# The vector engine takes its turns at the wide PSUM bank one product later

## What is computed

```python
# layer 0: x = e, xk = e;  layers 1 and 2: x = e, xk = the sum of the layer before, the same for all 256 columns
z = jnp.einsum('bfe,bge->bfge', x, xk).reshape(B, 256, E)
z = relu(einsum('bcl,oc->bol', z', Ws[i]) + bs[i])      # 16 outputs o for each column
z = sum(z, axis=-1)                                      # (B, 16)
h = concatenate([z of the three layers, dense_ctx])      # (2048, 64)
h = relu(h @ W_top1 + b_top1); h = relu(h @ W_top2 + b_top2); y = h @ W_top3
```

## Time and profile before

| what | value |
|---|---|
| time, median of 3 runs | 611.44 us (611.04 to 613.63) |
| the profiled execution | 614.28 us, span 612.5 us |
| granted TensorE clock, mean of the span | 0.989 |
| PE busy | 566.3 us, 92% |
| DVE busy | 494.5 us, 81% |
| ACT busy | 437.6 us, 71% |
| POOL busy | 463.1 us, 76% |

### The profile page before, as it was taken

How to read it: one execution, slowest core, us unless ns; L and a number is a source line. 1 busy time by engine, 2 the same in 40 slices (tenths; PEclk the granted TensorE clock), 3 DMA queues, 4 the chain that set the end, 5 groups by cost and what they waited for, 6 DMA issues and landing times.

```text
span 612.5 us, 18145 instructions
## 1 busy us (share of the span) xinstructions
PE 566.3 (92%) x7680; PEld 329.1 (54%) x7680; DVE 494.5 (81%) x220; ACT 437.6 (71%) x1234; POOL 463.1 (76%) x565
## 2 busy tenths in 40 slices
PE   1778889999999999999999999999999999999776
PEld 1334445555555565655556555555556565555444
DVE  5898899888888988888889888888899888887100
ACT  2466677768778776878878777887877786886542
POOL 5989888888878887888878888888878788862000
PEclk9999899999999999999999999999999999999978
DMA  4422222222222222222222122222222222210000
GB/s 98 115 76 73 62 62 71 61 62 63 61 62 63 61 63 63 61 63 61 63 63 65 58 64 62 60 63 61 63 64 63 68 61 59 59 45 1 1 1 2
DMA packets 14788, 35.89 MB, mean 59 GB/s; under 512 B 5921, under 2 KB 6305, under 8 KB 14689
## 3 DMA queue, kind: packets, MB, share of 16 engines
q0 software_dynamic: 12288, 33.57, 19.3%
q1 hardware_dynamic: 2418, 1.16, 0.8%
HBM read 34.70 MB, written 0.01 MB: 57 GB/s over the span
## 4 chain that ended last, share of the span: by engine, by line
PE 68%; DVE 20%; issue 7%; ACT 3%; POOL 2%; DMA 0%; SPq 0%; DVEq 0%; POOLq 0%; ACTq 0%
PE sum_ps L521 29%; DVE prods L222 19%; PE turn_ps L501 9%; PE outer_ps L564 9%; PE wide_ps L585 7%; PE sum_ps L541 5%; PE wide_ps L576 4%; PE outer_ps L559 3%; ACT relu_k L431 2%; POOL emb L262 2%; PE sum_ps L536 1%; PE wide_ps L593 1%; PE sum_ps L547 0%; PE sum_ps L533 0%; DMA id_lim<-id_limits 0%
## 5 line engine op out<-in xcount | busy, mean ns | idle before, releaser
L222 DVE TENSOR_TENSOR prods<-turn_ps,emb_t 128x3360 f32<-128x3360 f32 x128 | 462.2, 3646 | 11.8 <-ACT emb_t L404 8.9
L262 POOL DMA_INDIRECT emb<-tables,rows_sb x256 | 252.1, 985 | 44.9 <-issue 31.1
L521 PE MATMUL sum_ps<-prods,w_sb 128*32 128x272 f32 x4096 | 267.1, 400 | 2.5 <-POOL prods L222 2.3
L521 PEld LDWEIGHTS sum_ps<-prods,w_sb 128*32 128x32 f32 x4096 | 126.0, 110 | 94.0 <-issue 14.5
L421 ACT ACTIVATE relu<-sum_ps,bias_sb 128x120 f32<-128x120 f32 x256 | 91.8, 370 | 100.8 <-PE sum_ps L521 96.6
L272 POOL TENSOR_TENSOR prods<-emb_t 128x256 f32<-128x256 f32 x128 | 94.8, 741 | 53.8 <-ACT emb_t L404 50.3
L431 ACT ACTIVATE relu_k<-outer_ps 128x2048 f32<-128x2048 f32 x64 | 120.9, 1889 | 4.5 <-PE outer_ps L564 4.4
L501 PE MATMUL turn_ps<-ident_sb,emb 128*128 128x128 f32 x512 | 90.7, 295 | 29.7 <-DVE prods L222 10.9
L403 ACT COPY emb_t<-turn_ps 128x512 f32<-128x512 f32 x128 | 76.1, 595 | 44.2 <-PE turn_ps L501 36.2
L501 PEld LDWEIGHTS turn_ps<-ident_sb,emb 128*128 128x128 f32 x512 | 55.1, 143 | 88.8 <-issue 49.0
L411 ACT ACTIVATE prods<-emb_t 128x512 f32<-128x512 f32 x128 | 83.0, 649 | 0.1
(11 more groups left out here) (41 smaller groups left out, 269.2 us busy)
## 6 DMA issues: line engine op xcount, KB each, us to landing
emb<-tables,rows_sb POOLq DMA_INDIRECT x256
w_sb<-w_top SPq DMA_DIRECT2D x1, 512.0 KB
ids_sb<-ids_t SPq DMA_DIRECT2D x1, 128.0 KB, 2.0
h<-dense_t SPq DMA_DIRECT2D x1, 128.0 KB
w_sb<-w_top SPq DMA_DIRECT2D x1, 128.0 KB
ident_sb<-ident SPq DMA_DIRECT2D x1, 64.0 KB
w_sb<-w_cols SPq DMA_DIRECT2D x1, 64.0 KB
wp_sb<-w_proj SPq DMA_DIRECT2D x1, 32.0 KB
```

The costliest lines, as they stand in the source:

```text
L222: eng.tensor_tensor(out, every, shifted, ALU.mult).then_inc(done, 1)
L262: nc.gpsimd.indirect_dma_start(out=emb[:, k % EMB_RING, t * E:(t + 1) * E], out_offset=None, in_=tables, in_offset=bass.IndirectOffsetOnAx ...
L521: last = nc.tensor.matmul(sum_ps[s * 2 * F:(s + 1) * 2 * F, 0:SUM_COLS], w_sb[:, c, odd, :], x[:, c, 2 * s + odd, :, :], start=c == 0 and ...
```

## The change

Two constants are raised by one slot. `turn_proj(g)` stands after `products` of slot 12 instead of slot 11, `reduce_fields(0, g)` after that of slot 16 instead of 15, and `reduce_fields(1, g)` after that of slot 21 instead of 20. No instruction is added or taken away, and no other engine's program is touched; what each semaphore counts is the same.

```diff
-PROJ, Z0_FIN, TURN_P, Z0_DIAG, Z0_SUM = 10, 9, 11, 9, 10
+PROJ, Z0_FIN, TURN_P, Z0_DIAG, Z0_SUM = 10, 9, 12, 9, 10
 Z_BUILD = (11, 15)
 ROUNDS = (12, 16)
 FOLD = (14, 19)
-REDUCE = (15, 20)
+REDUCE = (16, 21)
```

## The result

The changed kernel took 623.82 us (median of 4 runs, 623.65 to 624.13) against 611.76 for the kernel before in the same series (4 runs, 611.04 to 613.63): ratio 1.0193, 95% interval 1.0169 to 1.0217, 12.1 us slower. The forecast was 618.3: 623.8 lies inside its range, but the loss was put too small, 6.8 us against 12.1. The profiled execution has a span of 622.0 us, 9.5 more than the profile of before; that one profile lay above all of its runs (614.28 us against 611.04 to 613.63), which is why the medians are further apart than the spans.

A forecast was written before the change was run, and what follows sets the result against it. The prediction took TensorE to bound the kernel: 10.1 us lost in groups 1 to 14 less 3.3 gained in group 0 is 6.8 us slower, 611.44 + 6.8 = 618.3 us, range 609.5 to 625.

The forecast's parts named there:

- What bounds the kernel: Whole kernel: TensorE, busy 92% of the span, sets the time; the DVE's large waits belong to an engine with time to spare.
- The wait that takes the place of the one removed: Slots 11 and 15: TensorE's last sum matmul waits for the wide bank; slot 11's release at 376.03, slot 15's at 393.26.
- Slot 11, net 0.77 us: Slot 11, groups 1 to 14: new wait of 0.93 us for the transpose, less the old 0.16 us in slot 12.
- Slot 15, net -0.05: Slot 15, groups 1 to 13: new wait of 0.26 us for the sum, less the old 0.31 us in slot 16.
- No slack elsewhere: Middle groups: neither new wait feeds on slack that an earlier one made, since ScalarE's copies hang on TensorE's sums.
- Sum of groups 1 to 14: Groups 1 to 14: 13 x 0.72 + 0.77 = 10.1 us lost, bounds 3.8 and 15.5 us.
- Group 0: Group 0: gaps of 1.82 and 1.80 us and slow sums (1.69 us) go; 3.3 us gained, bounds 1.8 and 5.3.
- The limit that I named there: Group 0: POOL reaches 82.9 us, and the sums of slot 17 can't start before that, which limits the 5.31 us gain.
- POOL's late spread: Slot 15: POOL's `z_spread(1, g)` waits some 2 us longer for the moved sum; cost zero, without cover up to 1 us a group.
- the second sum: Slot 20 to 21: the sum is ready before its first reader either way; cost and gain zero, without cover 0.42 us a group.
- (1): Rival, slots 11 and 15: new waits don't bite and only the old ones go; 9.6 us faster, 601.8; chance 0.10.
- (3): Rival, sums after the new wait: TensorE's clock falls, 1.69 us per set in 14 groups; 30.5 us slower, 642; chance 0.04.

The follow-up runs named there:

- the second pair of profiles: The kernel before and the changed kernel, both unchanged, run and profiled once more on one chip: 611.84 us and 623.47 us.

## Why the prediction was right, and where it was too small

- **What bounds the kernel**: right. TensorE's order does; the DVE's waits for TensorE before the transposes and the sums fell from 84.5 to 31.4 us in all, and the kernel got no faster.
- **The wait that takes the place of the one removed**: right in place and in time. The release in slot 11 was put at 376.03 on a slot that began at 372.87, 3.16 us into it; it was 379.41 - 376.25 = 3.16. The copy of ScalarE, the product and the transpose set it.
- **Slot 11, net 0.77 us**: too small, 1.01 measured. This is the term that was mis-sized. I had counted the wait from 375.1, the start of the last batch of matmuls, on the ground that "the array is free" after it. But the held matmul has a pass in each of the last two batches; in the trace of before its first pass starts at 374.87 and its second at 375.10. The first is what is held: it moved from 374.87 - 372.87 = 2.00 us into the slot to 3.16, by 1.16 us and not 0.93. The fold is cut into the same column groups and shifts with it: it started 3.17 us into the slot instead of 2.44, 0.73 late, and then took 2.29 us to the next turn instead of 1.85, another 0.44; together 1.17, less the old wait of 0.16 that is 1.01. With the wait moved behind the sums the 0.44 vanished (5.46 to 5.02 us), which shows it. My upper bound by the weights, 0.97, was nearer.
- **Slot 15, net -0.05**: it was +0.15. Here too I had taken the second pass (393.0); the first started at 392.77, 2.40 us into the slot, and now starts 2.89 us into it, 0.49 late. The sums end 0.52 us late, against 0.26 in the forecast, and the old wait was 4.41 - 4.04 = 0.37, not 0.31. With the wait behind the sums no wait was left at all.
- **No slack elsewhere**: slots 16 to 18 gave back 0.15 us, which I had not seen.
- **Sum of groups 1 to 14**: 10.1 forecast, 12.7 in the trace. **Group 0**: 3.3 forecast, 3.38 in the trace. The limit that I named there held: POOL's last blocks of step 17 end at 82.68 us against my 82.9, and the sums of slot 17 start at 82.79 (both rows stand above). On the way TensorE waited 0.62 us in slot 12 and 1.00 us in slot 16 for ScalarE's reading of the sums, which I had not seen; POOL, which had no gap from 66.4 us on, would have held it back without them. But that the gain came out at 3.3 is in part luck: 1.69 us of it were the slow sums, which the second pair of profiles does not have (1.85 us gained).
- **The median**: 6.8 us forecast, 12.1 measured. Of the 5.3 us missing, the trace of the first pair has 2.7 (9.5 us between the spans). The rest lies between that profile of before and its median, 614.28 against 611.76 us: I took the gain of group 0 from an execution with slow sums and added it to the median of executions most of which may not have had them. The second pair fits this, with 1.85 us gained in group 0 and 11.4 us between the spans; how many of the timed executions have the slow sums isn't on record.
- **POOL's late spread, the second sum, the tail**: nothing, as said. The run with the second sum alone shows 0; no run has the late spread alone, but TensorE's matmuls of line 521 wait for POOL only once in the whole span, 2.6 us at the start (2.3 before).
- **The rivals**: (1) needed a release 1.1 us earlier and did not occur. (3) did not occur: there are no sums of 3.7 us in the middle. The Trainium skill (TensorE: Matmul & The Clock Gate, "A second HAM failure mode: psum-queue depth-cycling") describes a clock that swings when TensorE idles shortly between groups of matmuls; this trace doesn't show it, with idle gaps of 0.54 us in each group and a granted clock of 1.00 from 368 to 416 us.

Of the 0.99 us a group, 0.87 hang on the place of TensorE's wait and 0.1 to 0.2 on the late evacuation itself (34.99 against 34.84 us with the wait at the user in both, on different chips). That remainder is itself a balance: with the wait at the user slot 11 is still 5.02 - 4.45 = 0.57 us longer than in the old order, and slots 15 to 18 give most of it back.

## What to carry to other kernels

A consumer's wait for its producer is cheap while the producer has other work; before it is moved, look for who needs the buffer next on the engine that bounds the kernel, and work out the release from the last input to arrive and not from the wait that is to vanish. Put a wait for a shared buffer directly ahead of the buffer's user: anything held behind it that did not need the buffer is added to the wait. And an order that is good for all groups but the first can be wrong in the first, where the work that covers it does not exist yet.

## What the runs showed of the hardware

- A matmul into a quarter of the columns that is held alone costs more than its place in a batch: the batches of four passes of the sums start 0.23 us apart, and one held matmul had its two passes 0.25 us apart (379.41 and 379.67) and stretched the fold behind it by 0.44 us.
- The same program took different times on three chips: the kernel before took 607.05 us (17 runs, 604.35 to 609.29) on one, 612.39 (29 runs, 609.68 to 616.35) and 613.82 (12 runs, 610.55 to 615.92) on the others. In the profile that stands for it on the first, the DVE got the result of the fold of slot 14 1.98 us behind the fold's start (350.11 - 348.13), not 2.22 (390.74 - 388.52). Why is not settled; in the middle groups an execution repeats its value to within 0.05 us.
- The same gap does not always lower TensorE's clock. The gap of 1.82 us before slot 12 of group 0 stands in six profiles, all of kernels with the old transpose; the sums behind it ran slow in three (3.73, 3.41 and 3.44 us) and in 2.04 us in the other three. In the run with the fold moved and the old transpose, gaps of 1.82 to 1.83 us stand in all of groups 0 to 14: slow sums followed in groups 0 and 1, sums of 2.04 us in the other thirteen. In the earlier trace rows, where the clock fell to 0.53, it cost 1.69 us on top of the gap. What decides it is not settled.
- Executions of one kernel differ with the granted clock: of the kernel before in its series of 29, the two at 0.981 took 616.3 us and the two at 0.997 took 609.7 and 609.8.
